# Differential attention and a ternary FFN on one core: one gelu pass per pair of query tiles, and work moved from VectorE to GpSimd

## What is computed

```python
x = x + attention(layernorm(x))
x = x + ffn(layernorm(x))

# attention: 32 query heads and 16 key heads of 16, 8 value heads of 32, rope, causal mask
probs = softmax(scores)                       # 32 maps, in 16 pairs
diff = probs[:, :, 0] - lambda_full * probs[:, :, 1]
attn = rmsnorm(diff @ v) * subln_weight * (1 - LAMBDA_INIT)
return attn @ Wo.T

# ffn: weights cut to -1, 0, 1
h = gelu(x @ w1_q.T + b1, approximate=False)  # 2048 wide
return h @ w2_q.T + b2
```

## Time and profile before

| what | value |
|---|---|
| timed, median of 3 | 4142.19 us (4137.09 to 4144.37) |
| the profiled execution, its own time | 4130.02 us |
| its span, first to last instruction | 4128.2 us |
| mean granted TensorE clock | 0.938 |
| busy share | PE 81%, DVE 80%, ACT 70%, POOL 43% |

### The profile page before, as it was taken

The page is one execution under the profiler, slowest core; times in us unless marked ns, Lnnn a source line. Parts: engine busy times, 40 slices in busy tenths (PEclk is TensorE's granted clock), DMA queues, the critical chain, the costliest instruction groups (busy, mean ns, idle before and its releaser), DMA issues. The chain is left out here.

```text
span 4128.2 us, 85771 instructions
## 1 busy us (share of the span) xinstructions
PE 3339.5 (81%) x24230; PEld 2075.6 (50%) x24230; DVE 3291.2 (80%) x5317; ACT 2895.7 (70%) x6800; POOL 1780.4 (43%) x2322
## 2 busy tenths in 40 slices
PE   4787888888878888878887888878888788787888
PEld 2455555555545555545554555545455455454545
DVE  6888878888788887888778887788877888788784
ACT  4577766777667776677766777677776777667774
POOL 1255443454334543345443544435443444434444
PEclk7799999999999999999999999999999999999999
DMA  4000011100101001100011010110001010010100
GB/s 149 29 28 21 20 34 35 34 15 30 32 28 34 18 29 38 32 23 29 21 34 34 20 34 16 35 34 30 25 23 37 25 34 20 30 36 21 32 20 23
DMA packets 146896, 128.70 MB, mean 31 GB/s; under 512 B 66656, under 2 KB 117728, under 8 KB 145888
## 3 DMA queue, kind: packets, MB, share of 16 engines
q1 hardware_dynamic: 146400, 122.79, 9.1%
HBM read 67.61 MB, written 55.12 MB: 30 GB/s over the span
## 5 line engine op out<-in xcount | busy, mean ns | idle before, releaser
L632 ACT ACTIVATE E<-SP_,NM 128x256 f32<-128x256 f32 (+7 forms) x2048 | 1524.8, 745 | 968.7 <-DVE NM L801 512.9
L793 DVE TENSOR_REDUCE NM<-SP_ 128x1 f32<-128x896 f32 (+3 forms) x1024 | 1031.4, 1016 | 271.6 <-PE SP_ L1020 266.4
L1019 PE MATMUL SP_<-KST,QST 96*128 96x512 f16 (+3 forms) x3072 | 832.4, 342 | 414.6 <-ACT E L632 362.1
L820 DVE SCALAR_TENSOR_TENSOR E<-E,CC 128x512 f32<-128x512 f32 (+7 forms) x1024 | 975.1, 952 | 76.2 <-POOL CC L540 57.9
L1031 PE MATMUL DP<-ident,E 128*128 128x128 f32 x3328 | 578.6, 289 | 146.4 <-DVE E L820 135.9
L1019 PEld LDWEIGHTS SP_<-KST,QST 96*128 96x128 f16 x3072 | 272.1, 101 | 711.1 <-ACT E L632 522.1
L537 POOL TENSOR_TENSOR RP<-SUM,minus 128x1 f32<-128x1 f32 x512 | 311.7, 609 | 696.4 <-ACT E L632 686.7
L644 ACT ACTIVATE DT<-DP 128x512 f32<-128x512 f32 (+3 forms) x1024 | 526.2, 514 | 88.5 <-PE DP L1031 80.7
L1031 PEld LDWEIGHTS DP<-ident,E 128*128 128x128 f32 x3328 | 388.5, 148 | 297.0 <-issue 171.6
L801 DVE TENSOR_REDUCE NM<-SP_ 128x2 f32<-128x1024 f32 (+3 forms) x512 | 419.0, 818 | 125.0 <-PE SP_ L1020 111.3
L1076 PE MATMUL F<-X2H,W1Q 128*128 128x256 f16 x1984 | 491.5, 285 | 9.0 <-DVE SQ L930 8.4
(11 more groups left out here) (131 smaller groups left out, 5125.4 us busy)
## 6 DMA issues: line engine op xcount, KB each, us to landing
scratch<-SPL SPq DMA_DIRECT2D x65, 576.0 KB, 2.8
QST<-scratch SPq DMA_DIRECT2D x390, 64.0 KB, 2.4
X<-in_x SPq DMA_DIRECT2D x66, 256.0 KB, 2.7
out<-SQ SPq DMA_DIRECT2D x63, 256.0 KB, 2.0
KST<-scratch SPq DMA_DIRECT2D x390, 32.0 KB, 1.9
DT<-in_w1T SPq DMA_DIRECT2D x2, 1024.0 KB, 12.1
DT<-in_w2T SPq DMA_DIRECT2D x2, 1024.0 KB, 8.6
E<-in_wqT SPq DMA_DIRECT2D x1, 1024.0 KB, 8.9
```

The costliest lines, as they stand in the source:

```text
L632: act.activation(dst, score_out(i, 2 * n + k, w), ACT.Exp, bias=NM[:, (2 * u + k) % 8:(2 * u + k) % 8 + 1], scale=1.0, accum_out=SUM[:, i ...
L793: nc.vector.tensor_reduce(NM[:, m:m + 1], score_out(i, 2 * n + k, P * (i + 1)), AX.X, ALU.max, negate=True).then_inc(max_ready, 1)
L820: nc.vector.scalar_tensor_tensor(out=E1[:, u % 4, 0:w], in0=E2[:, u % 2, 0:w], scalar=CC[:, u % 4:u % 4 + 1], in1=E1[:, u % 4, 0:w], op0=A ...
L1019: pe.matmul(SP_[:, k[a // 512], 0:n], q, KST[0:ROWS, a // P:(a + n) // P, kk, :], start=True, stop=not last)
```

## The change

There are four parts. **Gelu:** HP now holds all 16 hidden tiles, both gelu passes stand together at half-step 0 of the even tile, between one pair of table loads; the pass at half-step 14 of the odd tile is gone. HL is written in place, into the first half of each row of HP. **Splits and second product:** all eight splits stand in the even tile, at half-steps 3, 4, 5, 9, 13, 15, 17 and 18; the lump at half-step 1 is gone; the second product's first rows are spread over half-steps 13 to 20, two hidden tiles each, its other rows over 21 to 30; DVE's first residual sum moves from 17 to 20. **Coefficients:** POOL makes them from t = 3 on. **Low rows:** for t = 5, 6 and 7 ACT writes a second, fp32 copy WT of M, and POOL makes WTL from WT and WTH; PE's next user of M then waits for ACT's copies alone, and the low passes of the projections wait for POOL.

```diff
+LOW_TILE = 5
+RATIO_TILE = 3
+RATIO_HEADS = N_U - H * RATIO_TILE
...
-GELU_ODD, GELU_EVEN = 14, 0
-SPLIT_ODD, SPLIT_EVEN = (16, 18, 20, 22), (2, 4, 6, 8)
+GELU_AT = 0
+SPLIT_AT = (3, 4, 5, 9, 13, 15, 17, 18)
 SQUARE = 9
-W2_LUMP, W2_REST, W2_NEXT = 1, (10, 7), (18, 13)
-OUT_AT = (17, 31)
+W2_AT = ((13, 8), (21, 10))
+OUT_AT = (20, 31)
...
+        WT = sb("WT", [P, D], F32)
...
-        HP = sb("HP", [P, GELU_F, 2 * P], F32)
+        HP = sb("HP", [P, FT, 2 * P], F32)
         HH = sb("HH", [P, FT, 2 * P], F16)
-        HL = sb("HL", [P, FT, 2 * P], F16)
+        HL = HP[:, :, :].rearrange("p a b -> p (a b)").bitcast(F16).rearrange("p (a b) -> p a b", a=FT)[:, :, 0:2 * P]
...
+            def turned_low(ready, n, done):
+                after(pool, ready, n + 1)
+                pool.tensor_tensor(WTL[:, :], WT[:, :], WTH[:, :], ALU.subtract).then_inc(done, 1)
...
-                    if hs % 2 == 0 and old and old[1] >= 4:
+                    if hs % 2 == 0 and old and old[1] >= RATIO_TILE:
                         ratio(*old)
...
+                ins = act.activation(WTH[:, :], M[:, :], ACT.Copy)
+                if twice:
+                    ins = act.activation(WT[:, :], M[:, :], ACT.Copy)
+                ins.then_inc(xt_ready, 1)
...
-            def gelu(q, j):
-                after(act, hp_ready, 8 * q + 4 * j + 4)
-                act.activation(HP[:, :, :], HP[:, :, :], ACT.Gelu).then_inc(gelu_done, 1)
+            def gelu(q):
+                after(act, hp_ready, 8 * q + 8)
+                for j in range(0, FT, GELU_F):
+                    act.activation(HP[:, j:j + GELU_F, :], HP[:, j:j + GELU_F, :], ACT.Gelu).then_inc(gelu_done, 1)
...
-                if i >= 4:
-                    after(dve, ratio_ready, b * N_U + 2 * u - N_U + 2)
+                if i >= RATIO_TILE:
+                    after(dve, ratio_ready, b * RATIO_HEADS + u - H * RATIO_TILE + 1)
...
-                    hold(pe, h_ready, 8 * q + 4)
                     hold(pe, hp_ready, 8 * q + 8)
                     hold(pe, o_sum, 2 * q + j)
+                if j == 0:
+                    hold(pe, h_ready, 8 * q + fs[-1] // 2 + 1)
...
-                            after(pe, xt_low, nb + 1)
+                            after(pe, xt_ready if T.low_by_pool else xt_low, nb + 1)
```

More of the change, by code:

```diff
@@ L158, in __init__ @@
         self.raw = kind == "first"
+        self.low_by_pool = t >= LOW_TILE
     def before(self, n):
@@ L178, in second_product @@
             return None
-        if hs == W2_LUMP:
-            return 0, range(0, GELU_F)
-        for j, f0, (at, n) in ((0, GELU_F, W2_REST), (1, 0, W2_NEXT)):
+        for j, (at, n) in enumerate(W2_AT):
             if at <= hs < at + n:
-                return j, range(f0 + (FT - f0) * (hs - at) // n, f0 + (FT - f0) * (hs - at + 1) // n)
+                return j, range(FT * (hs - at) // n, FT * (hs - at + 1) // n)
         return None
@@ L554, in pool_work @@
                             pool.tensor_copy(V[:, 0, :], VST[:, :]).then_inc(v0_moved, 1)
+                        if hs == XT_LOW and T.low_by_pool:
+                            turned_low(xt_ready, T.nb, xt_low)
                         if hs == Q_ROPE:
@@ L571, in pool_work @@
                                                ALU.mult).then_inc(an_ready, 1)
+                        if hs == ANT_LOW and T.low_by_pool:
+                            turned_low(ant_ready, T.nf, ant_low)
                         if hs == LN2_STATS:
@@ L577, in pool_work @@
                         split(T.nb, 1)
-                    if T.w1 and hs in SPLIT_ODD:
-                        hidden_split(T.pair, SPLIT_ODD.index(hs))
-                    if T.w2 and hs in SPLIT_EVEN:
-                        hidden_split(T.pair, 4 + SPLIT_EVEN.index(hs))
+                    if T.w2 and hs in SPLIT_AT:
+                        hidden_split(T.pair, SPLIT_AT.index(hs))
                     if T.w2 and hs in OUT_AT:
@@ L679, in act_work @@
                             after(act, m_kv, nb + 1)
-                        act.activation(WTH[:, :], M[:, :], ACT.Copy).then_inc(ant_ready, 1)
+                        ins = act.activation(WTH[:, :], M[:, :], ACT.Copy)
+                        if T.low_by_pool:
+                            ins = act.activation(WT[:, :], M[:, :], ACT.Copy)
+                        ins.then_inc(ant_ready, 1)
                     if T.finish and hs == LN2_TURN:
@@ L690, in act_work @@
                         after(act, f1_ready, n + 1)
-                        after(act, h_ready, n - 3)
                         for f in (2 * k, 2 * k + 1):
-                            ins = act.activation(HP[:, f % GELU_F, :], F[:, 2 * P * (f % 2):2 * P * (f % 2) + 2 * P],
+                            ins = act.activation(HP[:, f, :], F[:, 2 * P * (f % 2):2 * P * (f % 2) + 2 * P],
                                                  ACT.Identity, bias=b1c[:, f:f + 1], scale=1.0 / XS)
                         ins.then_inc(hp_ready, 1)
-                    if T.w1 and hs == GELU_ODD:
-                        gelu(T.pair, 0)
-                    if T.w2 and hs == GELU_EVEN:
-                        gelu(T.pair, 1)
+                    if T.w2 and hs == GELU_AT:
+                        gelu(T.pair)
             def abs_chunk(j, k):
@@ L878, in dve_work @@
                             normalise(0, slot, nb, xn_ready)
-                        if hs == XT_LOW:
+                        if hs == XT_LOW and not T.low_by_pool:
                             turned_low(xt_ready, nb, xt_low)
@@ L907, in dve_work @@
                             nc.vector.tensor_scalar(VE[:, :], MS[:, :], 1.0 / DV, EPS, ALU.mult, ALU.add).then_inc(ms_ready, 1)
-                        if hs == ANT_LOW:
+                        if hs == ANT_LOW and not T.low_by_pool:
                             turned_low(ant_ready, nf, ant_low)
@@ L992, in transposes, with project @@
                 ins.then_inc(done, 1)
-            def project(w, c0, passes, done):
+            def project(w, c0, passes, done, low_part=None):
                 for k in passes:
+                    if k == 2 * KD and low_part:
+                        after(pe, *low_part)
                     j, part = (k // 2, k % 2) if k < 2 * KD else (k - 2 * KD, 0)
@@ L1085, in second_product @@
                 if fs[0] == 0:
-                    hold(pe, h_ready, 8 * q + 4)
                     hold(pe, hp_ready, 8 * q + 8)
                     hold(pe, o_sum, 2 * q + j)
+                if j == 0:
+                    hold(pe, h_ready, 8 * q + fs[-1] // 2 + 1)
                 for f in fs:
-                    if f == GELU_F and j == 0:
-                        hold(pe, h_ready, 8 * q + 8)
                     for hp in (HH, HL):
```

60 lines of the change are left out of this document (28 added, 32 removed).

## The result

The changed kernel takes 4200.74 us (median of four timed runs, 4200.37 to 4201.83), the kernel before 4140.26 us beside it. The ratio is 1.0149, with a 95% interval from 1.0136 to 1.0161: it is slower by 60 us, where 24 us less were forecast.

What follows compares the result with a forecast made beforehand. No engine is full; DVE and PE lead in turn, losing stretches where all wait for one. Terms -111 + 57 + 41 + 10 - 34 - 19 + 23 + 10 give -24 us: 4142.2 to 4118 us, range 4048 to 4188 (8 times in 10).

Steps and rivals of the forecast that it cites:

- block: Even tile's start: a second gelu pass between the same two table loads adds 1.91 us, +57 us over 30 passes.
- lump: Even tiles: 16 matmuls, free under the gelu before, move to half-steps 13 to 30 and partly cost time, +41 us.
- clock: Behind even tiles' gelu stop: PE granted half clock, while odd stops go; net loss 1.4 us per looped entry, +10 us.
- splits: Even tiles: four more POOL splits make POOL 4.0 us late in tile 4; +23 us, between -10 and +80.
- low rows: Tiles 5 to 7: DVE saves 2.1 us per tile, ACT writes two more copies; 0.8 us per tile, -19 us.
- coefficients: Tile 3: DVE loses two small operations per head, 8.5 us per tile, half of it counted; -34 us.
- Odd gelu: Odd tiles: removing the gelu wins DVE's idle time there, 14.2 us per entry, 11.7 in the first; -111 us.
- Tail: End of the kernel: eight splits instead of four before the last two hidden tiles, with PE's work queued behind; +10 us.
- "port" rival: Coefficients and low rows: what DVE saves it waits for POOL's reads, both terms go; 4171 us, chance 0.12.
- GpSimd late: Rival: second-group splits hold up coefficients and PE, 3 us in each even tile; 4178 us, chance 0.22.

Runs made afterwards that it cites:

- e3: Changed kernel with both the coefficients of tile 3 and the low rows of tiles 5 to 7 given back to DVE: 4201.65 us (ratio 1.0153).
- e7: Changed kernel with 26 unused PE matmuls at half-step 1 of each even tile, run while ACT is in the gelu: 4179.01 us (ratio 1.0115).
- e4: Changed kernel with the residual sum at half-step 22 instead of 20 and the second product's other rows starting at 23: 4174.58 us (ratio 1.0088).
- e6: Changed kernel with splits at half-steps 3 to 8, 10 and 13, and the second product's first rows at 11 to 18: 4124.43 us (ratio 0.9976).
- e8: Changed kernel with POOL's low part of each split cut to 16 of 256 columns, and PE reading the high part twice: 4144.29 us (ratio 1.0029).
- e1: Changed kernel with the coefficients of tile 3 given back to DVE: 4202.37 us (ratio 1.0157).
- e16: Kernel before, with only the coefficients of tile 3 moved to POOL: 4145.64 us (ratio 1.0020).
- e2: Changed kernel with the low rows of tiles 5, 6 and 7 given back to DVE: 4204.49 us (ratio 1.0164).
- e5: e4 with its last five splits earlier, all eight at half-steps 3 to 8, 10 and 13: 4205.84 us (ratio 1.0178).

## Why the prediction was wrong

The forecast of 4118 us fell short by 83; between the two traced executions, of which the tiles are, it is 94 (4200.4, where 4106 was forecast for one like the traced). From the kernel before, the even tiles cost 28.0 us an entry where the terms came to 17.9 (7.6 for the block, 5.7 lump, 1.4 clock, 4.0 splits, less 0.8 for tile 6's low rows): seven times 10.1 is 71 us. The odd tiles gave 19.2 where the terms came to 21.1: 13 us. The first entry rose by 2.8 where the terms came to -12 (-11.7 for the gelu, 3.8 block, 1.0 lump, 1.5 splits, -6.7 for coefficients and low rows): 15 us. (These are medians of entries, so their sum, 99, is not exactly 94.)

By stretches (medians), the even tiles' 28 us are 7.2 at the four stops, 3.6 in the half-steps 2 to 5 behind them, 10.2 from 13 to 21, 5.8 from 21 to 26 and 1.4 elsewhere. So most of the shortfall lies from half-step 13 on: 17 us there, where the terms for lump and splits came to 9.7. Point by point:

- **Odd gelu, -111 us: right in mechanism, too small.** With the other parts undone (e3) the odd tiles fall by 20.0 us an entry, 140 us in the loop, where 15.2 with the splits were taken. No idle stretch of DVE in tile 3 is over 1.6 us now, where the earlier trace rows had 3.26. Tiles 5 and 7 gained most, and PE's own busy time fell in them, with a granted clock from 0.93 to 0.97 and from 0.90 to 0.93 in the fourth looped entry.
- **Block, +57 us: right.** The start of the even tiles is 1.8 us longer in each.
- **Lump and clock, +41 and +10 us: the clock too small, the lump not measured by itself.** The granted clock in half-steps 2 to 5 was 0.76, 0.61, 0.61 and 0.78 in tiles 0, 2, 4 and 6. These stretches grew by 3.6 us an entry, 25 in the loop, where 10 were taken. Covering the stop gave back 22 us in e7 (14 by the ratios), with the clock in tile 4 still not at 1.00.
- **Splits, +23 us: the step that failed most.** The prediction named POOL's 4.0 us of lateness in tile 4, PE's wait at half-step 20 and the residual sum behind it, and priced only the first: 2 us in tile 4, 0.5 in tile 6. It put DVE's wait at the residual sum at nothing. Measured between half-steps 13 and 21 are 4.8 us in tile 4, and in every even tile a 3.4 us wait of DVE's in-order queue. Moving the sum away (e4), the second product with its splits (e6) or leaving most of POOL's low parts out (e8) gave back 26, 76 and 56 us. Rows before the change that bore on it are the earlier trace rows and the table of half-steps itself: a product that ends at 20 and a sum at 20, where the kernel before had 16 and 17. I read the wait's length from POOL alone and did not ask how far DVE's list runs ahead of PE's.
- **Coefficients, -34 us: wrong.** The earlier trace rows show 8.5 us of DVE's work, and that DVE was busiest in the tile. But a coefficient by POOL comes later: DVE waited as long as it had worked (e1, e16), and tile 3 fell by 4.0 us, where 7 or so were forecast. The "port" rival had this result, both terms gone, by another mechanism: of the 5.7 us per tile 3, waiting is 4.7 and longer joins 1.1. The prediction also says that the earlier trace rows agree with a port kept by whoever issues first. They show the join losing 0.87 us beside the multiply, but the join began first, by 0.03 us (2119.81 and 2119.84); so they bear out the contention and not that order.
- **Low rows, -19 us: wrong.** 0 within the measurement (e2, e3). PE's wait for WTL fell from 82.9 us in the earlier trace rows to 57.8, and the tiles kept their length; which wait took its place was not traced.
- **Tail, +10 us: right in size, in part by luck.** The last tile and the tail together went from 145.4 to 150.3 us, while a tile 7 fell by 5.8: 10.7 us. The prediction had POOL at work without a wait, by the splits' own length. In fact POOL stood for 4.7 us in the tail, since its fourth split stands behind the square of the attention rows, which waits for DVE's rows:

```profile
4137.51 1.04 POOL L571 TENSOR_TENSOR SQ<-TOK 128x512 f32<-128x512 f32 x1 [4.71 <-DVE TOK L909]
```

With the same eight splits earlier, the last tile and the tail take 142.0 us (e5) instead of 148.4 (e4).

The result, 4201, is nearest to the rival *GpSimd late* (4178). With its 3 us in each even tile the even tiles' terms would come to 25.9 us an entry, where 28.0 were measured. Its condition was that PE's second product waits for splits, or DVE's joins for coefficients, by more than 1 us in each even tile. PE waited for splits 16.0 us in all, which is too little. DVE's joins waited 5.2 us in a tile 4 and 2.9 in a tile 6 (3.0 and 1.0 before), but in tiles 0 and 2, which lost 12 of the 28 us, GpSimd makes no coefficients. So the condition holds in two even tiles of four. What tiles 0 and 2 lost came back in part with the earlier product (e6) and, in tile 0, the covered stop (e7), and little of it with GpSimd relieved (e8). Of all 118.7 us of waits for coefficients (57.9 before), 40.9 are tile 3's.

What stays open: how the 76 us of e6 divide between its earlier splits and its earlier product; how much of what e8 gave back is GpSimd's lateness and how much its contention with DVE's joins; and why tile 3 does not get shorter although its join ends 2.3 us behind the exponential where it is 2.9 in e1 (medians). A version with a coefficient that costs neither engine anything was not tried.
